# Cross-attention scores of one head on one half of the partitions

## The chip, the core and the metric

The kernel runs on one core of one Trainium2 chip. The time is the device time of one execution in microseconds. PE is TensorE (matmuls), PEld its weight loads, DVE VectorE, ACT ScalarE, POOL GpSimd, SP the engine that issues most DMAs. All five run their own instruction streams and wait for each other by semaphores.

## The reference

One decoder layer on x of 32 batch rows x 112 tokens x 256 channels: a first attention (a delta rule with an MLP), then cross-attention to a context of 375 keys, then a routed MLP with six experts. The change touches the middle part alone:

```python
Q, K, V = split(query @ wq.T), split(key @ wk.T), split(value @ wv.T)   # 16 heads of 16 channels
scores = einsum('bhqd,bhkd->bhqk', Q, K) / sqrt(16)
scores = where(mask == 1, -1e9, scores)
out = einsum('bhqk,bhkd->bhqd', softmax(scores), V)                     # then w_out
```

## The kernel before

The order of the instructions on each engine is written by hand; there is no scheduler. After the first attention (to about 500 us) comes the cross-attention, a loop over the batch rows (32 of them, three to a round of the hardware loop, `par` being the place in the round), then the routed MLP from about 1100 us.

**How a batch row goes through it.** Three rows are in work at once. While row b has its scores and weighted values, row b+1 (`nxt`) has the maxima of its scores, row b+2 (`far`) its projections of k, q and v, and row b-1 (`prev`) its last weighted values, its transposes and its output projection. `step(t, par)` in the stream of PE, ACT, DVE, POOL and SP writes one such mixed row.

**Exact products in fp32r.** Each of q and k is split in a high and a low part, and the score is hi·hi + hi·lo + lo·hi. SP copies the parts by DMA into stacks so that one matmul sums all three (`spread_heads`, L454 to L465). The stack `kst` holds a *pair* of heads on 96 partitions (3 terms x 2 heads x 16 channels) and 376 keys. The stack `qst` holds each head alone on the same 96 partitions with zeros at the other head's, so that products with the pair's keys give one head. Partition 96 holds ones in `kst` and the negated row maximum in `qst`, which `spread_max` (L467 to L470) brings by a DMA from `negm`.

**Slots.** The scores come transposed, keys on partitions, in 12 slots `q` of a row: 3 pieces of 125 keys x 4 groups of 4 heads, each 448 columns in one of PSUM banks 0, 1, 2. For a slot PE runs one bf16 product that adds a large negative number at masked keys (`mask_scores`, L968 to L976; it waits until the exponentials have freed the bank), then two products of 224 columns, one for each pair of heads (`score`, L978 to L983). ACT takes the exponential of the slot (`exponentials`, L1431) into one of six buffers `pr`, and `weighted_values` (L985 to L997) multiplies it with the values: four heads, on four strips of 32 output partitions of bank 6; each of these fp32 matmuls is two instructions in the trace. These run in three groups of four slots.

**Maxima.** The maximum over the keys of each head of the next row: PE computes 112 x 376 scores of one head (`row_max`, L950 to L961) into bank 4 or 5, DVE adds the mask's bias and reduces (`maxima`, L1822 to L1831). The 16 heads are spread over slots 0 to 7 by the table `MAXIMA` (L80). PE transposes the 16 maxima (`transpose_max`), ACT negates them (`negate_max`), SP spreads them.

**Clearing.** POOL clears `qst` and sets `kst`'s last partition to one, once for each of the three stacks (`clear_stack`, L568 to L572), the first inside the first attention, the other two at its end.

Of the kernel before, what the change touches and what calls it, by code (L numbers as in the profile page):

```python
# [40 lines left out]
P = 128  # L41
# [28 lines left out]
PROBS = 6  # L70
# [3 lines left out]
ROWS = 3 * 2 * HD  # L74
# [5 lines left out]
MAXIMA = ((0, 1, 0, 0), (1, 1, 1, 0), (1, 1, 0, 1), (0, 1, 0, 0), (1, 1, 0, 0), (1, 1, 1, 0), (1, 0, 0, 1), (0, 1, 0, 0))  # L80
# [36 lines left out]
def decoder_layer(nc, io, out):  # L117
    with ExitStack() as ctx:
# [74 lines left out]
        with ExitStack() as scope:  # L193
# [116 lines left out]
        def pair(stack, n):  # L310

            return stack[:, n % PPC, n // PPC]

        def head(stack, hd):

            return pair(stack[:, hd % 2], hd // 2)

        def both(stack, n):

            return stack[:, :, n % PPC, n // PPC]  # L320
# [28 lines left out]
        def heads_at(q, place):  # L349

            n = sum(sum(x) for x in MAXIMA[:q]) + sum(MAXIMA[q][:place])
            return range(n, n + MAXIMA[q][place])

# [16 lines left out]
        def filled(stack, t):  # L370

            return {"kst": 48, "qst": 96}[stack] * (t + 1)
# [29 lines left out]
        def _(sp):  # L402
# [51 lines left out]
            def spread_heads(t, par):  # L454

                b = t * RB + par
                for src, r, ready in ((khi, 0, "k_hi"), (khi, 2, "k_hi"), (klo, 1, "k_lo")):
                    sp.wait_ge(s2[ready], DC * (b + 1))
                    dst = kst[par][r:ROWS:3]
                    sp.dma_start(dst.bitcast(F32), src[:].bitcast(F32)).then_inc(s2[f"kst{par}"], 16)  # L460
                for src, r, ready in ((qhi, 0, "q_hi"), (qhi, 1, "q_hi"), (qlo, 2, "q_lo")):
                    sp.wait_ge(s2[ready], b + 1)
                    for e in range(2):
                        dst = qst[par][3 * e + r:ROWS:6, e]
                        sp.dma_start(dst.bitcast(F32), src[cols(e, P // 2)].bitcast(F32)).then_inc(s2[f"qst{par}"], 16)  # L465

            def spread_max(t, par):  # L467
                b = t * RB + par
                sp.wait_ge(s2["negm"], b + 1)
                sp.dma_start(qst[par][ROWS:ROWS + 1].bitcast(F32), negm[:].bitcast(F32)).then_inc(s2["negm_in"], 16)  # L470
# [70 lines left out]
        def _(pool):  # L541
# [26 lines left out]
            def clear_stack(i):  # L568
                nc.gpsimd.memset(qst[i][0:ROWS].bitcast(F32), 0.0).then_inc(s2["cleared"], 1)
                pool.wait_ge(s2["cleared"], 2 * i + 1)  # L570
                nc.gpsimd.memset(kst[i][ROWS:ROWS + 1].bitcast(F32), 1.0).then_inc(s2["cleared"], 1)
                pool.wait_ge(s2["cleared"], 2 * i + 2)  # L572

            def stack_constants():

                pool.wait_ge(s["y_ps"], G)
                clear_stack(0)
# [64 lines left out]
            pool.wait_ge(s["x_mlp"], G)  # L642
            clear_stack(1)
# [65 lines left out]
        def _(pe):  # L709
# [240 lines left out]
            def row_max(t, par, heads):  # L950

                n = t * RB + par
                for hd in heads:
                    if hd == 0:
                        pe.wait_ge(s2[f"qst{par}"], filled("qst", t))
                        pe.wait_ge(s2[f"kst{par}"], filled("kst", t))
                        if not is_row(n, 0):
                            pe.wait_ge(s2["negm"], n)
# [9 lines left out]
            def mask_scores(t, par, q):  # L968

                b = t * RB + par  # L970
                if q == 0:
                    pe.wait_ge(s2["negm_in"], 16 * (b + 1))
# [5 lines left out]
            def score(t, par, q, i):  # L978

                n = HPB // 2 * (q % HPB) + i  # L980
                mm = pe.matmul(bank[q % 3][0:KP, cols(i, 2 * T)], pair(kst[par], n)[:, cols(q // HPB, KP)], both(qst[par], n), start=False, stop=True, skip_group_check=True)  # L981
                if i == HPB // 2 - 1:
                    mm.then_inc(s2["sc_ps"], 1)  # L983

            def weighted_values(t, par, q):  # L985
# [6 lines left out]
                for i in range(HPB):  # L992
                    hd = HPB * (q % HPB) + i
                    row = 2 * HD * i
                    mm = pe.matmul(bank[6][row:row + 2 * HD, cols(hd // HPB)], vaug[par][:, c3, hd], pr[q % PROBS][:, i],  # L995
# [29 lines left out]
            def step(t, par, first=False, following=2):  # L1025

                prev, nxt, far = ahead(t, par, -1), ahead(t, par, 1), ahead(t, par, 2)
                for q in range(SLOTS):

                    maxima = following >= 1 and q < len(MAXIMA)  # L1030
                    mask_scores(t, par, q)
                    for i in range(HPB // 2):
                        score(t, par, q, i)
                        if maxima:
                            row_max(*nxt, heads_at(q, i))
                    if q % HPB == 1 and q > HPB:
                        for earlier in range(q - HPB - 1, q - 1):
                            weighted_values(t, par, earlier)
                    elif q == 1 and not first:
                        for earlier in range(SLOTS - HPB, SLOTS):  # L1040
                            weighted_values(*prev, earlier)
                    if maxima:
                        row_max(*nxt, heads_at(q, 2))
                    if q in (1, 2) and following >= 2 and not first:
                        project_k(*far, q - 1)
                    if q == 3 and not first:
                        transpose_o(*prev)
                    if q == 4 and following >= 2:
                        transpose_h(*far)
                    if q == 5 and not first:  # L1050
                        transpose_on(*prev)
                    if q == 6 and following >= 2:
                        project_q(*far)
                    if q == 7 and not first:
                        project_out(*prev)
                    if maxima:
                        row_max(*nxt, heads_at(q, 3))
                    if q == 8 and following >= 1:
                        transpose_max(*nxt)
                    if q == 8 and following == 0:  # L1060
                        transpose_group(0)
                    if q == 8 and following >= 2:
                        project_v(*far, 0)
                        project_v(*far, 1)


# [199 lines left out]
        def _(act):  # L1266
# [188 lines left out]
            def step(t, par, first=False, following=2, context=True):  # L1455
                prev, nxt, far = ahead(t, par, -1), ahead(t, par, 1), ahead(t, par, 2)
                for q in range(SLOTS):
                    exponentials(t, par, q)
                    if q == 1 and not first:
                        copy_pv(*prev)  # L1460
                    if q in (1, 2) and following >= 2:
                        high_k(*far, q - 1)
                    if q == 4 and following >= 2:
                        copy_h(*far)
                    if q == 5 and not first:
                        copy_on(*prev)
                    if q == 6 and following >= 2:
                        high_q(*far)
                    if q == 8 and following >= 1:
                        negate_max(*nxt)  # L1470
                    if q == 8 and following >= 2:
                        copy_v(*far, 0)
                    if q == 9 and following >= 2:
                        copy_v(*far, 1)
                    if q == 9 and context:
                        high_context(*ahead(t, par, 3))
                    if q == 9 and following == 0:
                        keep_h(0)
# [125 lines left out]
        def _(dve):  # L1604
# [217 lines left out]
            def maxima(t, par, heads):  # L1822
                n = t * RB + par
                for hd in heads:
                    if hd == 0:
                        dve.wait_ge(s2["flags"], n + 1)
                    if hd >= 2:
# [3 lines left out]
                                                   op0=ALU.add, op1=ALU.max, accum_out=head(smax, hd).unsqueeze(1)).then_inc(s2["smax"], 1)  # L1831
# [26 lines left out]
            def step(t, par, first=False, following=2, norm=True):  # L1858
                prev, nxt, far = ahead(t, par, -1), ahead(t, par, 1), ahead(t, par, 2)
                for q in range(SLOTS):  # L1860
                    if following >= 1 and q < len(MAXIMA):
                        for place in range(3):
                            maxima(*nxt, heads_at(q, place))
                    if q in (2, 3) and following >= 2:
                        low_k(*far, q - 2)
                    if q == 4 and not first:
                        normalise_heads(*prev)
                    if q == 7 and following >= 2:
                        low_q(*far)
                    if following >= 1 and q < len(MAXIMA):  # L1870
                        maxima(*nxt, heads_at(q, 3))
                    if q == 7 and not first:
                        add_row(*prev)
# [278 lines left out]
```

## Time and profile before

| | us |
|---|---|
| median of 3 runs | 1502.91 (1502.6 to 1508.58) |
| the profiled execution | 1504.27 |
| its span | 1502.4 |
| PE busy | 1315.5 (88%) |
| DVE busy | 907.6 (60%) |
| ACT busy | 646.6 (43%) |
| POOL busy | 420.7 (28%) |

The page cuts the span in 40 slices of 37.6 us and gives the busy share and the granted TensorE clock of each; the cross-attention is slices 14 to 29. Matmuls overlap in the array, and their ends are modelled: the duration of one is longer than what it takes of PE's time in a full queue. That is read from the distance between starts or ends.

### The profile page before, as it was taken

Reading aid. Unit: us, or ns where it says so; the run is one execution under the profiler, and the core shown is the slowest. Engines: PE = TensorE matmul, PEld = TensorE weight load, DVE = VectorE, ACT = ScalarE, POOL = GpSimd, SP = SyncE. Lnnn points to the kernel's source line nnn. Section 1 sums busy time; section 2 is a strip of 40 time slices with the busy share of each in tenths; the row PEclk is TensorE's granted clock in tenths of the full one; section 3 lists DMA queues with packets and bytes.
Section 4 is the critical chain, followed back from the end, with each engine's and each line's share of the span. In section 5 each row is a group of like instructions: output and inputs, shape, how many; then the busy total and the mean of one; then the engine's idle time right before and its main releaser. Section 6 shows DMA issues by size and latency. Waiting matters only on the chain.

```text
span 1502.4 us, 33730 instructions
## 1 busy us (share of the span) xinstructions
PE 1315.5 (88%) x11138; PEld 1182.9 (79%) x11138; DVE 907.6 (60%) x2823; ACT 646.6 (43%) x1474; POOL 420.7 (28%) x387
## 2 busy tenths in 40 slices
PE   4999999999897699999999999999975518988987
PEld 4888998998786588888888888888865417877887
DVE  4676567557545366666666666666557534544567
ACT  3533434334332255555555555555542204544532
POOL 2233223224312311111111111111006662323453
PEclk9999999999998699999999999999985558999999
DMA  7699100000002445454555555554304322322264
GB/s 182 149 236 247 32 0 0 0 0 0 18 13 49 126 110 114 115 116 120 120 120 119 119 122 119 120 120 117 79 9 126 116 76 70 101 80 86 89 160 138
DMA packets 117837, 143.96 MB, mean 96 GB/s; under 512 B 24112, under 2 KB 101280, under 8 KB 117744
## 3 DMA queue, kind: packets, MB, share of 16 engines
q1 hardware_dynamic: 111024, 127.21, 36.1%
q0 software_dynamic: 6160, 15.69, 3.2%
q8 instruction: 43, 0.70, 0.2%
q14 instruction: 34, 0.28, 0.1%
q10 hardware_dynamic: 576, 0.07, 0.0%
HBM read 75.61 MB, written 42.15 MB: 78 GB/s over the span
## 4 chain that ended last, share of the span: by engine, by line
PE 59%; issue 14%; POOL 9%; DVE 8%; SPq 2%; DMA 2%; ACT 2%; another core or an unknown queue 0%; POOLq 0%; DVEq 0%; ACTq 0%
PE psum L725 19%; PE psum L961 7%; PE psum L995 5%; PE psum L976 5%; PE psum L981 5%; POOL routed_y L686 4%; POOL routed_h L671 3%; PE psum L846 2%; SPq L465 2%; PE psum L843 2%; PE psum L832 2%; PE psum L933 2%; PE psum L1022 2%; PE psum L714 1%; PE psum L1008 1%
## 5 line engine op out<-in xcount | busy, mean ns | idle before, releaser
L1830 DVE CUSTOM_DVE_ANT_0 junk<-psum,biasq 112x375 f32<-112x375 f32 x512 | 270.0, 546 | 116.5 <-PE psum L961 78.2
L1435 ACT ACTIVATE pr<-psum 125x448 f32<-125x448 f32 x384 | 202.7, 544 | 115.5 <-PE psum L981 107.1
L981 PE MATMUL psum<-qst,kst 97*125 97x224 f32 x768 | 225.8, 353 | 0.0
L961 PE MATMUL psum<-kst,qst 96*112 96x376 f32 x512 | 185.7, 371 | 12.4 <-DVE smax L1830 10.7
L981 PEld LDWEIGHTS psum<-qst,kst 97*125 97x125 f32 x768 | 146.2, 190 | 8.0
L976 PE MATMUL psum<-flagk,negbig 125*125 125x448 bf16 x384 | 139.0, 362 | 4.0 <-DMA qst<-negm 3.8
L566 POOL TENSOR_TENSOR rs<-rs,neg_half 112x1 f32<-112x1 f32 x32 | 18.3, 571 | 388.1 <-DVE rs L1808 388.1
L961 PEld LDWEIGHTS psum<-kst,qst 96*112 96x112 f32 x512 | 91.3, 179 | 41.9 <-DVE smax L1830 36.7
L686 POOL DMA_INDIRECT routed_y<-yb,yrow x61 | 59.3, 972 | 136.5 <-ACT yb L1565 134.8
L995 PE MATMUL psum<-pr,vaug 125*32 125x112 f32 x3072 | 93.7, 262 | 0.0
L995 PEld LDWEIGHTS psum<-pr,vaug 125*32 125x32 f32 x3072 | 70.3, 109 | 15.4 <-issue 6.1
L631 POOL TENSOR_SCALAR biasq<-maskq 112x375 f32<-112x375 int32 x32 | 56.0, 1749 | 89.8 <-PE psum L981 89.8
L1697 DVE TENSOR_TENSOR clo<-ctxT,chi 128x750 fp32r<-128x750 f32 x32 | 30.1, 941 | 81.1 <-ACT chi L1337 81.1
L2075 DVE TENSOR_TENSOR hidb<-sgb,psum 128x256 f32<-128x256 f32 x61 | 25.7, 421 | 88.2 <-ACT sgb L1550 83.7
L671 POOL DMA_INDIRECT routed_h<-h,slot x64 | 63.6, 993 | 36.5 <-DVE slot L1982 18.8
L1356 ACT COPY xq<-psum 112x224 f32<-112x224 f32 x96 | 32.6, 348 | 88.1 <-PE psum L832 85.6
L832 PE MATMUL psum<-tri,cT 112*112 112x112 f32 x384 | 48.4, 268 | 19.3 <-DVE triT L1711 10.8
L587 POOL TENSOR_TENSOR cT<-negT,masks_sb 112x448 f32<-112x448 f32 x48 | 61.2, 1303 | 7.9 <-DVE negT L1706 7.9
L832 PEld LDWEIGHTS psum<-tri,cT 112*112 112x112 f32 x384 | 44.5, 181 | 23.2 <-POOL cT L587 13.3
L976 PEld LDWEIGHTS psum<-flagk,negbig 125*125 125x125 bf16 x384 | 52.8, 137 | 12.4 <-issue 5.3
L1550 ACT ACTIVATE sgb<-psum 128x256 f32<-128x256 f32 x61 | 23.5, 385 | 75.4 <-PE psum L1124 75.4
L714 PE MATMUL psum<-ident_sb,h 112*128 112x112 f32 x128 | 21.5, 330 | 38.8 <-DVE h L1855 25.9
(308 smaller groups left out, 3443.5 us busy)
## 6 DMA issues: line engine op xcount, KB each, us to landing
kst<-khi SPq DMA_DIRECT2D x64, 376.0 KB, 5.5
routed_h<-in_route_pad SPq DMA_DIRECT2D x6, 3640.0 KB, 41.1
kst<-klo SPq DMA_DIRECT2D x32, 376.0 KB, 6.7
ctxT<-in_ctxT SPq DMA_DIRECT2D x32, 375.0 KB, 5.2
hblk<-routed_h SPq DMA_DIRECT2D x61, 130.0 KB
qst<-qhi SPq DMA_DIRECT2D x128, 56.0 KB, 2.2
h<-routed_y SPq DMA_DIRECT2D x16, 448.0 KB, 5.2
stage<-in_e SPq DMA_DIRECT2D x21, 256.0 KB
```

The lines of the kernel that those rows point to most:

```text
L587: nc.gpsimd.tensor_tensor(cT[:, n], negT[:], over_rows(M_BT + 1 + n), op=ALU.mult).then_inc(s["cmask"], 1)
L631: nc.gpsimd.tensor_scalar(biasq[:, par, :], maskq[:], 1.0, -BIG, ALU.is_equal, ALU.mult)
L671: pool.indirect_dma_start(hbuf[:, :], to, h3[g % RINGS][:, j, :], None).then_inc(s3[f"scat{g % RINGS}"], 16)
L686: pool.indirect_dma_start(ybuf[:, :], to, yb[:, u], None).then_inc(s4[f"out{u}"], 16)
L725: mm = pe.matmul(to, st, mv, start=n == 0, stop=n == len(products) - 1)
L832: mm = pe.matmul(bank[6 + u][0:T, cols(j % 2)], cT[:, n, j], tri[:, j], start=True, stop=True)
L961: pe.matmul(bank[max_bank(n, hd)][0:T, 0:S2E], head(qst[par][0:ROWS], hd), pair(kst[par][0:ROWS], hd // 2), start=True, stop=True).then_in ...
L976: pe.matmul(bank[q % 3][0:KP, 0:GT], negbig[:], flags, start=True, stop=False, skip_group_check=True)
L981: mm = pe.matmul(bank[q % 3][0:KP, cols(i, 2 * T)], pair(kst[par], n)[:, cols(q // HPB, KP)], both(qst[par], n), start=False, stop=True, s ...
L995: mm = pe.matmul(bank[6][row:row + 2 * HD, cols(hd // HPB)], vaug[par][:, c3, hd], pr[q % PROBS][:, i], start=q == 0, stop=c3 == KC - 1, s ...
L1435: nc.scalar.activation(pr[q % PROBS][:].rearrange("k i q -> k (i q)"), bank[q % 3][0:KP, 0:GT], ACT.Exp, scale=1.0 / HD ** 0.5).then_inc(s ...
L1830: nc.vector.tensor_tensor_reduce(out=junk[:, hd % 2, :], in0=bank[max_bank(n, hd)][0:T, 0:S2], in1=biasq[:, par, :], scale=1.0, scalar=-3e ...
```

## The change

A stack holds one head on 48 partitions now (3 terms x 16 channels), even heads at partitions 0 to 47, odd ones at 64 to 111, in `kst` and `qst` alike. The row of ones and of the maximum is at partition 48 of each half. `qst` has no zeros and is half as large.

- A slot is four heads of one parity: slot q has parity q % 2 (`head_of`). Its scores are four products of 49 partitions x 112 columns instead of two of 97 x 224.
- Slots go two and two: both masks, four products of the even slot, four of the odd one (`scores`). All 12 slots are in six such blocks.
- The maxima of a pair of heads stand side by side, on two halves and in two banks, and wait once for all maxima before them; eight pairs stand between the blocks, and the table is gone.
- SP issues six DMAs for `kst` (three before) and two for `negm` (one before). The order of channels in `xwk` and of `xwo`'s rows follows.
- POOL sets 32 partitions of each half of `kst` to one, and clears nothing.
- The other steps of a row (projections, transposes, copies) are the same instructions at other places.

```diff
-ROWS = 3 * 2 * HD
+TERMS = 3
+ROWS = TERMS * HD
+HALF = 64
...
-                qst[i] = w2(f"qst{i}", [ROWS + 1, 2, PPC, DC, T], F32R)
-                kst[i] = w2(f"kst{i}", [ROWS + 1, PPC, DC, S2E], F32R)
+                qst[i] = w2(f"qst{i}", [P, PPC, DC, T], F32R)
+                w2(f"gap_q{i}", [P, PPC, DC, T])
+                kst[i] = w2(f"kst{i}", [P, PPC, DC, S2E], F32R)
...
+        def rows_of(e, first, n):
+
+            return slice(HALF * e + first, HALF * e + first + n)
+
+        def head(stack, hd, rows):
+
+            n = hd // 2
+            return stack[rows_of(hd % 2, 0, rows), n % PPC, n // PPC]
+
+        def head_of(q, i):
+
+            n = HPB * (q % HPB // 2) + i
+            return 2 * n + q % 2
...
-                    dst = kst[par][r:ROWS:3]
-                    sp.dma_start(dst.bitcast(F32), src[:].bitcast(F32)).then_inc(s2[f"kst{par}"], 16)
+                    for e in range(2):
+                        dst = kst[par][rows_of(e, HD * r, HD)]
+                        sp.dma_start(dst.bitcast(F32), src[cols(e, P // 2)].bitcast(F32)).then_inc(s2[f"kst{par}"], 16)
...
-                nc.gpsimd.memset(qst[i][0:ROWS].bitcast(F32), 0.0).then_inc(s2["cleared"], 1)
-                pool.wait_ge(s2["cleared"], 2 * i + 1)
-                nc.gpsimd.memset(kst[i][ROWS:ROWS + 1].bitcast(F32), 1.0).then_inc(s2["cleared"], 1)
-                pool.wait_ge(s2["cleared"], 2 * i + 2)
+                for e in range(2):
+                    nc.gpsimd.memset(kst[i][rows_of(e, HALF // 2, HALF // 2)].bitcast(F32), 1.0).then_inc(s2["cleared"], 1)
+                    pool.wait_ge(s2["cleared"], 2 * i + e + 1)
...
+                else:
+                    pe.wait_ge(s2["smax"], HEADS * n + heads[0])
                 for hd in heads:
...
-                    if hd >= 2:
-                        pe.wait_ge(s2["smax"], HEADS * n + hd - 1)
-                    pe.matmul(bank[max_bank(n, hd)][0:T, 0:S2E], head(qst[par][0:ROWS], hd), pair(kst[par][0:ROWS], hd // 2), start=True, stop=True).then_inc(s2["max_ps"], 1)
+                    pe.matmul(bank[max_bank(n, hd)][0:T, 0:S2E], head(qst[par], hd, ROWS), head(kst[par], hd, ROWS), start=True, stop=True).then_inc(s2["max_ps"], 1)
...
-                n = HPB // 2 * (q % HPB) + i
-                mm = pe.matmul(bank[q % 3][0:KP, cols(i, 2 * T)], pair(kst[par], n)[:, cols(q // HPB, KP)], both(qst[par], n), start=False, stop=True, skip_group_check=True)
-                if i == HPB // 2 - 1:
+                hd = head_of(q, i)
+                mm = pe.matmul(bank[q % 3][0:KP, cols(i)], head(kst[par], hd, ROWS + 1)[:, cols(q // HPB, KP)], head(qst[par], hd, ROWS + 1), start=False, stop=True, skip_group_check=True)
+                if i == HPB - 1:
                     mm.then_inc(s2["sc_ps"], 1)
...
+                def maxima(n):
+                    if following >= 1:
+                        row_max(*nxt, range(2 * n, 2 * n + 2))
+
+                def scores(q):
                     mask_scores(t, par, q)
-                    for i in range(HPB // 2):
+                    mask_scores(t, par, q + 1)
+                    for i in range(HPB):
                         score(t, par, q, i)
...
+                    for i in range(HPB):
+                        score(t, par, q + 1, i)
```

PE's whole row is now, in this order: maxima 0; k projection 0 (of `far`); scores 0 and 1; maxima 1; weighted values 8 to 11 of `prev`; scores 2, 3; maxima 2; k projection 1; maxima 3; `transpose_o`; scores 4, 5; maxima 4; `transpose_h`; weighted values 0 to 3; `transpose_on`; maxima 5; scores 6, 7; maxima 6; q projection; output projection; scores 8, 9; maxima 7; v projection; `transpose_max`; scores 10, 11; weighted values 4 to 7.

On PE, in the loop of the cross-attention, slots 2 and 3 of a row stood like this before (the second half of the k projection lies between them; 125x224 is a score product, 112x376 a maximum, 125x448 a mask):

```order
L976 MATMUL psum<-flagk,negbig 125x448
L981 MATMUL psum<-qst,kst 125x224
L960 REGISTER_ALU
L961 MATMUL psum<-kst,qst 112x376
L981 MATMUL psum<-qst,kst 125x224
L960 REGISTER_ALU
L961 MATMUL psum<-kst,qst 112x376
L725 MATMUL psum<-chi,wxk_hi 128x376 x2
L725 MATMUL psum<-clo,wxk_hi 128x376 x2
L725 MATMUL psum<-chi,wxk_lo 128x376 x2
```

The same place of the changed kernel:

```order
L979 MATMUL psum<-flagk,negbig 125x448
L977 REGISTER_ALU
L979 MATMUL psum<-flagk,negbig 125x448
L984 MATMUL psum<-qst,kst 125x112 x8
L962 REGISTER_ALU
L964 MATMUL psum<-kst,qst 112x376 x2
L728 MATMUL psum<-chi,wxk_hi 128x376 x2
L728 MATMUL psum<-clo,wxk_hi 128x376 x2
L728 MATMUL psum<-chi,wxk_lo 128x376 x2
L962 REGISTER_ALU
L964 MATMUL psum<-kst,qst 112x376 x2
```

Two masks stand together, the products are eight in a row with half the columns each, and the maxima come two at a time behind them. Products on half of the partitions (125x112, 112x376) border on ones over the whole array at three places here.

On SP, one row of the loop before:

```order
L460 DMA kst<-khi 32x4x752 x2
L460 DMA kst<-klo 32x4x752
L465 DMA qst<-qhi 16x4x224 x4
L465 DMA qst<-qlo 16x4x224 x2
L470 DMA qst<-negm 1x16x112
```

And now:

```order
L460 DMA kst<-khi 16x4x752 x4
L460 DMA kst<-klo 16x4x752 x2
L465 DMA qst<-qhi 16x4x224 x4
L465 DMA qst<-qlo 16x4x224 x2
L472 DMA qst<-negm 1x8x112 x2
```

The bytes are the same, in 14 transfers instead of 10.

## Rows read from the trace of the kernel before

**Rows 1.** The page: busy us, share of the span and instructions by engine.

```profile
PE 1315.5 (88%) x11138; PEld 1182.9 (79%) x11138; DVE 907.6 (60%) x2823; ACT 646.6 (43%) x1474; POOL 420.7 (28%) x387
```

**Rows 2.** The page: granted TensorE clock in 40 slices, in tenths.

```profile
PEclk9999999999998699999999999999985558999999
```

**Rows 3.** Stretches of 100 us: busy by engine, PEclk, DMA share, GB/s.

```profile
core 0: us, PE busy (x) PEld busy (x) DVE busy (x) ACT busy (x) POOL busy (x), PEclk, DMA share, GB/s
...
700.00:800.00 100.00, 98.65 (x1071) 87.40 (x1069) 66.09 (x226) 56.08 (x119) 17.35 (x16) 1.00 0.52 117
```

**Rows 4.** Groups of lines, shapes apart, 600 to 1056 us; columns as the page's part 5.

```profile
L1830 DVE CUSTOM_DVE_ANT_0 junk<-psum,biasq 112x375 f32<-112x375 f32 x391 | 206.3, 546 | 76.5 <-PE psum L961 65.4 <-issue 4.8
L981 PE MATMUL psum<-qst,kst 97*125 97x224 f32 x583 | 170.7, 350 | 0.0
...
L961 PE MATMUL psum<-kst,qst 96*112 96x376 f32 x391 | 140.0, 365 | 5.6 <-DVE smax L1830 5.6
...
L976 PE MATMUL psum<-flagk,negbig 125*125 125x448 bf16 x292 | 104.5, 358 | 1.4 <-DMA qst<-negm 1.4
L995 PE MATMUL psum<-pr,vaug 125*32 125x112 f32 x2336 | 71.1, 262 | 0.0
```

**Rows 5.** Timeline of PE, 816 to 819 us: start, duration, engine, line, count.

```profile
816.36 0.54 PE L981 MATMUL psum<-qst,kst 97*125 97x224 f32 x2
816.83 0.97 PE L995 MATMUL psum<-pr,vaug 125*32 125x112 f32 x32
817.73 0.40 PE L976 MATMUL psum<-flagk,negbig 125*125 125x448 bf16 x1
...
818.19 0.35 PE L976 MATMUL psum<-flagk,negbig 125*125 125x448 bf16 x1
818.22 0.54 PE L981 MATMUL psum<-qst,kst 97*125 97x224 f32 x2
818.60 0.35 PE L976 MATMUL psum<-flagk,negbig 125*125 125x448 bf16 x1
```

**Rows 6.** Timeline of PE: q projection, router products; then these alone by stretch.

```profile
811.19 1.05 PE L933 MATMUL psum<-h2T,xwq_sb 128*128 128x112 f32 x8
...
1110.99 1.65 PE L1083 MATMUL psum<-router_sb,hall 128*112 128x6 f32 x16
...
core 0: us, PE busy (x) PEld busy (x), PEclk, DMA share, GB/s
1110.90:1112.60 1.70, 1.61 (x16) 1.64 (x16) 1.00 0.00 0
```

**Rows 7.** Timeline of PE: maxima between products, 800 to 802 us.

```profile
800.80 0.34 PE L961 MATMUL psum<-kst,qst 96*112 96x376 f32 x1
800.97 0.27 PE L981 MATMUL psum<-qst,kst 97*125 97x224 f32 x1
801.47 0.42 PE L961 MATMUL psum<-kst,qst 96*112 96x376 f32 x1 [0.23 <-DVE smax L1830]
```

**Rows 8.** Timeline of PE's weight loads around weighted values, 801 and 817 us.

```profile
801.82 0.73 PEld L995 LDWEIGHTS psum<-pr,vaug 125*32 125x32 f32 x32 [0.18 <-ACT pr L1435]
802.72 0.17 PEld L961 LDWEIGHTS psum<-kst,qst 96*112 96x112 f32 x1 [0.17 <-DVE smax L1830]
...
817.73 0.13 PEld L976 LDWEIGHTS psum<-flagk,negbig 125*125 125x125 bf16 x1 [0.17 <-issue]
```

**Rows 9.** Waits, 600 to 1056 us: total us, times, longest us.

```profile
PE psum L961 <- DVE smax L1830: 5.6, 24, 0.2
```

**Rows 10.** Timeline: SP's issues of one row, and the mask product after them.

```profile
619.03 1.23 SPq L460 DMA_DIRECT2D kst<-khi  x2
620.48 0.55 SPq L460 DMA_DIRECT2D kst<-klo  x1
625.26 2.48 SPq L465 DMA_DIRECT2D qst<-qhi  x4
627.78 1.24 SPq L465 DMA_DIRECT2D qst<-qlo  x2
629.07 1.28 SPq L470 DMA_DIRECT2D qst<-negm  x1
...
631.69 0.40 PE L976 MATMUL psum<-flagk,negbig 125*125 125x448 bf16 x1 [0.32 <-DMA qst<-negm]
```

**Rows 11.** Timeline of POOL: one stack cleared, before the first rows.

```profile
496.34 1.59 POOL L569 MEMSET qst<- 96x1792 f32 x1 [19.67 <-DVE x_res L1692]
497.99 2.60 POOL L571 MEMSET kst<- 1x3008 f32 x1
```

More of the change, by code:

```diff
@@ L347, in ring_turn @@
             return 16 * (i // RINGS + 1)
-        def heads_at(q, place):
-            n = sum(sum(x) for x in MAXIMA[:q]) + sum(MAXIMA[q][:place])
-            return range(n, n + MAXIMA[q][place])
         def max_bank(row, hd):
@@ L370, in filled @@
         def filled(stack, t):
-            return {"kst": 48, "qst": 96}[stack] * (t + 1)
+            return 16 * 2 * TERMS * (t + 1)
         def split_weights():
@@ L642, in _ @@
             pool.wait_ge(s["x_mlp"], G)
+            pool.wait_ge(s2["flags"], 2)
             clear_stack(1)
@@ L992, in weighted_values @@
                 for i in range(HPB):
-                    hd = HPB * (q % HPB) + i
                     row = 2 * HD * i
-                    mm = pe.matmul(bank[6][row:row + 2 * HD, cols(hd // HPB)], vaug[par][:, c3, hd], pr[q % PROBS][:, i],
+                    mm = pe.matmul(bank[6][row:row + 2 * HD, cols(q % HPB)], vaug[par][:, c3, head_of(q, i)], pr[q % PROBS][:, i],
                                    start=q == 0, stop=c3 == KC - 1, skip_group_check=True)
@@ L1033, in step @@
                         score(t, par, q, i)
[L1034 to L1055, printed above, removed]
@@ new lines, in step @@
+                maxima(0)
+                if following >= 2 and not first:
+                    project_k(*far, 0)
+                scores(0)
+                maxima(1)
+                if not first:
+                    for q in range(SLOTS - HPB, SLOTS):
+                        weighted_values(*prev, q)
+                scores(2)
+                maxima(2)
+                if following >= 2 and not first:
+                    project_k(*far, 1)
+                maxima(3)
+                if not first:
+                    transpose_o(*prev)
@@ new lines, in step @@
+                scores(4)
+                maxima(4)
+                if following >= 2:
+                    transpose_h(*far)
+                for q in range(HPB):
+                    weighted_values(t, par, q)
+                if not first:
+                    transpose_on(*prev)
+                maxima(5)
+                scores(6)
+                maxima(6)
+                if following >= 2:
+                    project_q(*far)
+                if not first:
+                    project_out(*prev)
@@ L1067, in transpose_group @@
+                scores(8)
+                maxima(7)
+                if following >= 2:
+                    project_v(*far, 0)
+                    project_v(*far, 1)
+                if following >= 1:
+                    transpose_max(*nxt)
+                else:
+                    transpose_group(0)
+                scores(10)
+                for q in range(HPB, 2 * HPB):
+                    weighted_values(t, par, q)
             def transpose_group(g):
@@ L1456, in step @@
                 prev, nxt, far = ahead(t, par, -1), ahead(t, par, 1), ahead(t, par, 2)
[L1457 to L1478, printed above, removed]
+                if following >= 2:
+                    high_k(*far, 0)
+                exponentials(t, par, 0)
+                exponentials(t, par, 1)
+                if not first:
+                    copy_pv(*prev)
+                exponentials(t, par, 2)
+                exponentials(t, par, 3)
+                if following >= 2:
+                    high_k(*far, 1)
+                exponentials(t, par, 4)
+                exponentials(t, par, 5)
+                if following >= 2:
+                    copy_h(*far)
+                if not first:
+                    copy_on(*prev)
+                exponentials(t, par, 6)
+                exponentials(t, par, 7)
+                if following >= 2:
+                    high_q(*far)
+                exponentials(t, par, 8)
+                exponentials(t, par, 9)
+                if following >= 2:
+                    copy_v(*far, 0)
+                    copy_v(*far, 1)
+                if following >= 1:
+                    negate_max(*nxt)
+                if context:
+                    high_context(*ahead(t, par, 3))
+                if following == 0:
+                    keep_h(0)
+                exponentials(t, par, 10)
+                exponentials(t, par, 11)
             def last_mlp(m):
@@ L1859, in step, with largest @@
                 prev, nxt, far = ahead(t, par, -1), ahead(t, par, 1), ahead(t, par, 2)
[L1860 to L1873, printed above, removed]
+                def largest(n):
+                    if following >= 1:
+                        maxima(*nxt, range(2 * n, 2 * n + 2))
+                largest(0)
+                if following >= 2:
+                    low_k(*far, 0)
+                largest(1)
+                largest(2)
+                if following >= 2:
+                    low_k(*far, 1)
+                largest(3)
+                if not first:
+                    normalise_heads(*prev)
+                largest(4)
+                largest(5)
+                largest(6)
+                if following >= 2:
+                    low_q(*far)
+                if not first:
+                    add_row(*prev)
+                largest(7)
                 if norm:
```

43 lines of the change are left out of this document (14 added, 29 removed).

## The prediction

> **What bounds the kernel now.** I read first the busy times of the page: PE is busy 88% of the span, DVE 60% [rows 1]. Then the slices: the stretch from about 530 to 1090 us, the cross-attention over the 32 batch rows, holds a full TensorE clock [rows 2], and the table by stretches shows PE at 98.6 of 100 us there [rows 3]. The grouped lines from 600 to 1056 us hold 391 maxima products [rows 4], 16 to a batch row, so 24.4 rows in 456 us: 18.7 us a row. What the change rewrites on PE are the groups L981 (scores), L961 (maxima); L976 (mask) and L995 (weighted values) stand around them [rows 4]. DVE needs about 0.55 us for each maximum, 16 a row or some 9 us of 18.6, so it isn't the bound. The page's means of a matmul (350, 365 ns) are latencies; what one costs in a full queue is the distance between starts or ends in the timeline, and I price by that. At the granted clock of 1.00 a column takes 1/2.4 ns, so 448 mask columns take 0.187 us.
>
> **Score products.** A mask and its two products repeat every 0.41 us (818.19 to 818.60) [rows 5]. Less the mask that is 0.22, so 0.11 us a product, though its 224 columns stream in 0.093. What holds it is the weight load of 125 columns: router products that stream only 6 columns after loading 112 cost (1.65-0.17)/15 = 0.099 us each at full clock, and the q projection with 128 loaded and 112 streamed (1.05-0.26)/7 = 0.113 [rows 6]. For 125 columns that gives 0.110. The change doubles the products (24 to 48 a row), halves what each streams (112 columns, 0.047 us), and leaves each its own load of 125 columns. So a product on the same half still costs 0.11. Eight of them now follow two masks. Three gaps lie within the even four, three within the odd four: 6 x 0.11. Between the fourth even and first odd product the halves differ, so the odd load can run early: 0.05; the last streams 0.05. Sum 0.76 against 4 x 0.11 = 0.44 now: +0.32, six times a row +1.9, times 32 rows **+61 us**. Bounds: strictly one load after another, 0.88 a block, +84; loads of the two halves wholly beside each other, 0.44 a block, 0.
>
> **Maxima.** One costs 0.17 us today (800.80 to the next start at 800.97) [rows 7]. A pair now lies on two halves and two banks. No row of before shows two row halves at work together; the nearest shows four column strips at once: 32 instructions of L995 that would stream 0.093 us each alone (fp32 goes twice over its 112 columns: the q projection's 0.113 has the same stream) pass in (0.97-0.26)/31 = 0.023 us, a quarter, and their loads keep up [rows 5, 8]. So I take a pair at 0.19 instead of 0.34: -0.15, eight times, 31 rows: **-37 us**. Bounds: 0.17 a pair, -42; the second load (0.099) after the first, 0.27 a pair, -17. PE also stops once a row for the previous maximum, 5.6 us in 24.4 rows, 0.23 each [rows 9]. A pair now waits for both maxima before it, with everything else of PE queued behind that wait; but the pairs lie further apart: the tightest place, pairs 2 and 3, has a projection of k between them (six products of 376 columns, 1.0 us) against two maxima on DVE at 0.55 each [rows 4]; with the pair itself before it that just fits. **-7 us**.
>
> **Changes of the array's shape.** Around each group of L995 the weight loads stand idle 0.17 us, put down to issue or to a semaphore that was long there [rows 8]. In time of PE: from the end of the products (816.36+0.54 = 816.90) to the end of the next mask (817.73+0.40 = 818.13) lie 1.23 us; 32 instructions at 0.023 make 0.73, the mask 0.19. So entering and leaving cost 0.31, or 0.15 a change [rows 5]. Today a row has six such changes. Afterwards products on 49 or 48 partitions stand between ones on 112 to 128: counted in the order, 21 borders a row between whole array, half rows and column strips (every block of scores and every lone pair of maxima has two). The Trainium skill, "TensorEngine Tiling (Array Packing)", section Key Properties, says that a change of tiling mode, not of tile, drains TensorE. The trace agrees for column strips by the 0.17 us of idle load; for row halves nothing here shows it; with the rule the sum holds the next term, without it not. The nearest row being the column strips, I price all: 15 more x 0.15 = 2.25 us, 32 rows: **+72 us**. Bounds: 0 and about 90 (0.19, should each one cost like the dearer of the two sides).
>
> **Everything else.** The exponentials and mask products keep their number. DVE, ACT and POOL have free time, and their moved steps keep their slack while a row gets longer. The k stack goes out in six transfers instead of three, the negated maxima in two instead of one. An issue takes SP about 0.62 us, the one of negm 1.28 [rows 10]. SP is idle for much of a row; only negm is late already, by 0.32 us in the row shown. The new order has 16 transposed maxima later by a v projection (2.2 us) but two slots of scores, the weighted values, a pair and half a k projection follow before the next masks. I take 0 and keep +25 us as the bound (0.8 a row, one more small issue). POOL's clearing goes from 1.59 + 2.60 to two of 2.60 us a stack, +1.0; two such stacks hold up row 1's start, one more the stage before [rows 11], and SP's three further issues there cost 1.9: **+5 us**, bounds 0 and 7.
>
> **Sum.** 61 - 37 - 7 + 72 + 5 = +94 us. The profiled execution took 1504.27 us, 1.87 over its span, and gives 1598; the median of the runs, 1502.91, gives 1597, which I forecast.
>
> **Rivals.**
> 1. Changing between whole array and row halves is free. For it: no row shows its price. Then +94 - 72 = +22: 1525, between 1510 and 1555.
> 2. Faster: a queue that loads the odd half's weights under the even four wholly, and no price for changes. One mechanism, the two halves as two independent arrays, at each block of eight. Then products cost 0 more, maxima -42, the stop -7, start +5: -44, so 1459. It decides from a block of eight under 0.44 + 44/192 = 0.67 us, 0.084 a product. For it: column strips do run four at once. Against: there, neighbours in the order lie on different strips; here four neighbours lie on the same half, and matmuls would have to overtake. The Trainium skill, "TensorE: Matmul & The Clock Gate", section The mechanism, has matmuls start and end in program order, which speaks against it; the trace has no overtaking matmul. By that page the block would be no shorter than the 0.76 above.
> 3. No side by side at all to speak of: blocks 0.88 (+84), pairs 0.27 (-17), stop -7, changes +72, start +5: +137, 1640. For it: nothing shows row halves overlapping. A late negm on top of the forecast gives 1622 and counts here.
> 4. It nets to nothing: halfway between rivals 1 and 2 in the products (blocks of about 0.65 us) with free changes, 1503 within 7 us.
>
> **How the numbers follow.** Forecast 0.50 (own range 1560 to 1635), rival 1 0.20, rival 2 0.10, rival 3 0.15, nothing 0.05. A change under 0.5% (7.5 us) can't be told from none here. Slower: 0.50 + 0.20 + 0.15 and nearly all of it beyond 0.5%, less a little of rival 1's low end: 0.84. Within 0.5%: 0.05. Faster: rival 2 and that end, 0.11. The range drops rival 2 and the tail of rival 3: 1512 to 1645.
>
> **What would show it.** In the profile after: distances between starts of the scores products near 0.11 us within a four; the two maxima of a pair starting within some 0.02 us of each other (forecast) or 0.1 and more apart (rival 3); idle weight loads of 0.17 us at every border of shapes (forecast) or only around the weighted values (rival 1); a row of about 21.4 us (forecast), 19.2 (rival 1), 17.2 (rival 2). PE stays over 90% busy between 530 us and the end of the stage. The forecast is wrong if a block of eight takes under 0.6 us, or if the row's time grows by waits of PE for DVE, ACT or SP instead.

## The result and the profile after

| | before | changed |
|---|---|---|
| median, us | 1502.84 | 1646.39 (1639.83 to 1660.58, 4 runs) |
| ratio | | 1.096, interval 1.088 to 1.104 |
| profiled execution, its span | 1504.27, 1502.4 | 1643.54, 1641.7 |

The change costs 144 us; I had forecast 94, and the measured median lies 1.4 us above my range. The direction came true and two thirds of the amount, but not for the reasons given, so the parts matter more than the total. One of the four runs of `spread` below (1568.1 us) was in a slower state of the chip, and its ratio is that of the other three, whose median is 1555.47.

The page of the changed kernel, busy times and clock, answers to [rows 1, 2]:

```profile
PE 1412.3 (86%) x11906; PEld 1163.7 (71%) x11906; DVE 909.3 (55%) x2823; ACT 635.2 (39%) x1474; POOL 435.8 (27%) x387
...
PEclk9999999999976898997997999999965556999999
```

The clock no longer stands at full speed through the cross-attention. Four stretches of it (PE, PEld, DVE, ACT, POOL busy with counts, clock, DMA share, GB/s), against [rows 3]:

```profile
725.00:750.00 25.00, 23.30 (x256) 17.47 (x255) 15.07 (x52) 11.61 (x25) 3.84 (x4) 1.00 0.75 106
750.00:775.00 25.00, 23.67 (x190) 16.59 (x188) 10.12 (x34) 8.35 (x19) 3.77 (x3) 0.58 0.56 85
775.00:800.00 25.00, 24.74 (x253) 18.18 (x253) 14.55 (x50) 11.43 (x25) 3.81 (x3) 0.94 0.51 89
800.00:825.00 25.00, 22.59 (x275) 16.73 (x274) 14.58 (x48) 12.88 (x28) 5.73 (x5) 1.00 0.72 103
```

PE is busy for 94% instead of 98.6, the clock falls to 0.58 in one of four stretches, and the DMA engines are busy for 0.51 to 0.75 at 85 to 106 GB/s, where 0.52 moved 117 before.

The clock has two levels, 1.2 and 2.4 GHz, and 0.58 is a mixture of them. It fell right behind a stop of PE of 1.33 us (for q's low part, up to 753.43); then PE worked for 23.3 us without a pause at the lower level:

```profile
754.30:777.60 23.30, 23.30 (x149) 16.19 (x147) 9.07 (x34) 6.43 (x14) 0.46 (x1) 0.50 0.51 83
```

One row in PE's timeline (start, duration, line, count), against [rows 5, 7]:

```profile
802.04 0.97 PE L997 MATMUL psum<-pr,vaug 125*32 125x112 f32 x32
804.38 0.42 PE L964 MATMUL psum<-kst,qst 48*112 48x376 f32 x2 [1.37 <-DMA qst<-qlo]
804.73 0.62 PE L728 MATMUL psum<-chi,wxk_hi 128*128 128x376 f32 x2
805.19 0.51 PE L728 MATMUL psum<-clo,wxk_hi 128*128 128x376 f32 x2
805.53 0.51 PE L728 MATMUL psum<-chi,wxk_lo 128*128 128x376 f32 x2
...
806.35 0.66 PE L984 MATMUL psum<-qst,kst 49*125 49x112 f32 x8
806.83 0.39 PE L964 MATMUL psum<-kst,qst 48*112 48x376 f32 x2
...
812.02 0.66 PE L984 MATMUL psum<-qst,kst 49*125 49x112 f32 x8
812.76 0.42 PE L964 MATMUL psum<-kst,qst 48*112 48x376 f32 x2
...
815.58 0.66 PE L984 MATMUL psum<-qst,kst 49*125 49x112 f32 x8
816.39 0.43 PE L964 MATMUL psum<-kst,qst 48*112 48x376 f32 x2 [0.16 <-DVE smax L1859]
...
825.57 0.42 PE L964 MATMUL psum<-kst,qst 48*112 48x376 f32 x2 [1.35 <-DMA qst<-qlo]
```

Four things are to be seen. First, PE stands still for 1.37 us in front of the first pair of maxima, for the transfer of q's low part, and again 21.2 us later; that is a row at full clock, 18.69 before. Secondly, the block of eight products takes 0.48 us (806.35 to 806.83), not the 0.76 I had summed. Thirdly, two 376-column products of the k projection after a pair of maxima take 0.46 us to the next start (804.73 to 805.19) against 0.34 for the next two. Fourthly, at two places the pair of maxima starts 0.74 and 0.81 us after the eight products instead of 0.48: a wait for DVE of 0.26 and 0.33 us. The profile's own figure for it, 0.16, counts only from the modelled end of the products, which is later than the moment at which PE could have gone on.

PE's weight loads in the same block, against [rows 8], show how a block can be so short:

```profile
806.35 0.52 PEld L984 LDWEIGHTS psum<-qst,kst 49*125 49x125 f32 x8 [0.33 <-issue]
```

Eight loads of 125 columns lie in 0.52 us. Between 806.35 and 806.38 two of them have started, by 806.50 four: one load of each half every 0.11 us, (0.52-0.19)/3. So the even and the odd products run in pairs, though the program has four even ones first. In front of the block PE's loads stand idle for 0.33 us, which takes in the streaming of the second mask.

The waits of PE, 650 to 1130 us (total us, times, longest), against [rows 9]:

```profile
PE psum L964 <- DMA qst<-qlo: 26.0, 19, 1.8
...
PE psum L964 <- DVE smax L1859: 3.1, 20, 0.2
```

Of the page, part 5 (the last figure is the idle time put down to the transfer in the whole kernel):

```profile
L964 PE MATMUL psum<-kst,qst 48*112 48x376 f32 x512 | 113.4, 436 | 58.4 <-DMA qst<-qlo 45.7
```

And the transfers of 700 to 900 us in both kernels (count, KB each, median us from issue to landing). Before:

```profile
q1 hardware_dynamic: 18323, 23.22, 53.3%
...
kst<-khi SPq DMA_DIRECT2D x21, 376.0 KB, 5.8
...
qst<-qhi SPq DMA_DIRECT2D x44, 56.0 KB, 2.4
```

After:

```profile
q1 hardware_dynamic: 14950, 18.77, 61.9%
...
kst<-khi SPq DMA_DIRECT2D x32, 188.0 KB, 5.5
...
qst<-qhi SPq DMA_DIRECT2D x36, 56.0 KB, 5.0
...
qst<-qlo SPq DMA_DIRECT2D x18, 56.0 KB, 4.1
```

A transfer of q lands 5.0 us after its issue instead of 2.4. Engine time for a MB, over all transfers of the queue: 0.533 x 16 x 200 / 23.22 = 73 us before, 0.619 x 16 x 200 / 18.77 = 106 us after. The k transfers hold half of the bytes each and still take as long.

### The profile page after: what moved, and what is told of

Same layout as the page of the kernel before. It is cut to its first block and busy times, and to the rows that moved or that the text cites. A ratio compares the mean times of both kernels' runs of the same rounds, so it can differ in the third digit from the quotient of the medians.

```text
span 1641.7 us, 35236 instructions
## 1 busy us (share of the span) xinstructions
PE 1412.3 (86%) x11906; PEld 1163.7 (71%) x11906; DVE 909.3 (55%) x2823; ACT 635.2 (39%) x1474; POOL 435.8 (27%) x387
## 5 line engine op out<-in xcount | busy, mean ns | idle before, releaser
L1453 ACT ACTIVATE pr<-psum 125x448 f32<-125x448 f32 x384 | 188.0, 542 | 209.7 <-PE psum L984 197.6
L984 PEld LDWEIGHTS psum<-qst,kst 49*125 49x125 f32 x1536 | 112.5, 205 | 75.5 <-issue 75.5
L964 PE MATMUL psum<-kst,qst 48*112 48x376 f32 x512 | 113.4, 436 | 58.4 <-DMA qst<-qlo 45.7
L984 PE MATMUL psum<-qst,kst 49*125 49x112 f32 x1536 | 139.2, 302 | 0.0
L979 PE MATMUL psum<-flagk,negbig 125*125 125x448 bf16 x384 | 123.0, 406 | 0.0
L964 PEld LDWEIGHTS psum<-kst,qst 48*112 48x112 f32 x512 | 49.8, 187 | 90.9 <-DMA qst<-qlo 30.9
L633 POOL TENSOR_SCALAR biasq<-maskq 112x375 f32<-112x375 int32 x32 | 69.0, 2155 | 30.3 <-PE psum L984 30.3
L1428 ACT CAST khi<-psum 128x376 fp32r<-128x376 f32 x64 | 30.1, 472 | 113.6 <-PE psum L728 100.6
L1845 DVE TENSOR_TENSOR klo<-psum,khi 128x376 fp32r<-128x376 f32 x64 | 35.0, 549 | 48.1 <-ACT khi L1428 48.1
L728 PE MATMUL psum<-chi,wxk_hi 128*128 128x376 f32 x128 | 44.5, 433 | 13.7 <-DVE clo L1726 13.3
```

The lines of the kernel that those rows point to most:

```text
L633: nc.gpsimd.tensor_scalar(biasq[:, par, :], maskq[:], 1.0, -BIG, ALU.is_equal, ALU.mult)
L728: mm = pe.matmul(to, st, mv, start=n == 0, stop=n == len(products) - 1)
L964: pe.matmul(bank[max_bank(n, hd)][0:T, 0:S2E], head(qst[par], hd, ROWS), head(kst[par], hd, ROWS), start=True, stop=True).then_inc(s2["max ...
L979: pe.matmul(bank[q % 3][0:KP, 0:GT], negbig[:], flags, start=True, stop=False, skip_group_check=True)
L984: mm = pe.matmul(bank[q % 3][0:KP, cols(i)], head(kst[par], hd, ROWS + 1)[:, cols(q // HPB, KP)], head(qst[par], hd, ROWS + 1), start=Fals ...
L1453: nc.scalar.activation(pr[q % PROBS][:].rearrange("k i q -> k (i q)"), bank[q % 3][0:KP, 0:GT], ACT.Exp, scale=1.0 / HD ** 0.5).then_inc(s ...
```

## The experiments

**1. Spread the destinations.** The changed kernel writes each term of 16 channels to 16 adjacent partitions, the kernel before to every third (k) or sixth (q). `spread` puts the terms of a channel side by side within a half:

```diff
-                        dst = kst[par][rows_of(e, HD * r, HD)]
+                        dst = kst[par][HALF * e + r:HALF * e + ROWS:TERMS]
...
-                        dst = qst[par][rows_of(e, HD * r, HD)]
+                        dst = qst[par][HALF * e + r:HALF * e + ROWS:TERMS]
```

> The changed kernel with one edit: within each half the three terms of a channel lie side by side (partition 3 x channel + term), so that each transfer of 16 partitions is spread over 48 instead of lying on 16 adjacent ones. Theory N (writes to 16 adjacent partitions are slow, the queue of k and q transfers runs late, and PE waits about 1.3 us a row for qst and then gets a lower clock): PE's idle time before maxima 0 falls under 0.1 us a row, the clock stays at 1.00 between 600 and 1000 us, a row takes about 19.9 us, the kernel about 1545. Rival T (14 issues instead of 10 make it late) and rival O (the new order has k and q ready too late): nothing changes, about 1640.

Measured: 1558.85 us (median of four, 1544.72 to 1568.1; 1555.47 without the slowest), ratio to before 1.030 (1.024 to 1.037). A row takes 19.88 us (median distance of the starts of `transpose_max` between 600 and 1100 us; 18.69 in the kernel before, and so for every row below). The stretch of 700 to 800 us, the transfers, and what is left of the wait:

```profile
700.00:800.00 100.00, 98.51 (x1124) 72.32 (x1123) 63.19 (x215) 50.73 (x111) 19.01 (x15) 1.00 0.45 112
```
```profile
q1 hardware_dynamic: 17891, 22.40, 44.4%
...
kst<-khi SPq DMA_DIRECT2D x40, 188.0 KB, 3.7
...
qst<-qhi SPq DMA_DIRECT2D x43, 56.0 KB, 2.0
```
```profile
PE psum L964 <- DMA qst<-qlo: 1.2, 2, 0.8
```

The clock is back at 1.00, q lands in 2.0 us, a MB costs 0.444 x 16 x 200 / 22.40 = 63 us, and the wait came twice in 400 us. Theory N holds and T and O fall: the places of the destinations are 87 to 91 us of the 144 (against 1558.85 and 1555.47).

**2. The same from the other side.** `before_six` splits the k transfers of the kernel before into six and leaves them spread; `before_narrow` does the same and lays them on 16 adjacent partitions (the number of landings that PE waits for follows in both):

```diff
-                    dst = kst[par][r:ROWS:3]
+                    for e in range(2):
+                        dst = kst[par][48 * e + r:48 * e + 48:3]              # before_six
+                        dst = kst[par][32 * r + 16 * e:32 * r + 16 * e + 16]  # before_narrow
...
-                        dst = qst[par][3 * e + r:ROWS:6, e]
+                        dst = qst[par][32 * r + e:32 * r + 32:2, e]           # before_narrow
```

> The kernel before with its three k transfers a row split into six of 16 partitions each, still every third partition. Theory N: no change beyond 0.5%, 1503 to 1510, PE's wait for qst stays rare. Rival T: the number of transfers is what costs, over 1520.

> The same six transfers, but each on 16 adjacent partitions (terms one after another in blocks of 32 partitions), q on every second of 32. Theory N: engine time per MB of the DMAs goes up as in the changed kernel (by a third or more against before_six), the landing of q goes from about 2.4 to 4 us or more; the spare time of about 1 us a row is used up, so 1520 to 1580. Rival T or O: as before_six.

Measured: `before_six` 1502.6, ratio 0.999 (0.997 to 1.001); `before_narrow` 1575.13, ratio 1.047 (1.043 to 1.051). The number of transfers costs nothing that can be told, their place 5%. The narrow one's transfers and wait, 600 to 1000 us:

```profile
q1 hardware_dynamic: 33763, 42.55, 69.0%
...
kst<-klo SPq DMA_DIRECT2D x38, 188.0 KB, 8.4
```
```profile
PE psum L977 <- DMA qst<-negm: 28.9, 19, 2.5
```

Here the wait shows at negm's transfer, which stands behind q's in the queue: 28.9 us in 19 rows, 1.52 a row; its row takes 20.32 us, 1.63 more than before. A MB costs 0.69 x 16 x 400 / 42.55 = 104 us against 68 in `before_six` (0.502, 47.55 MB).

**3. The order of the products.** `spread_alternate`:

```diff
                     for i in range(HPB):
                         score(t, par, q, i)
-                    for i in range(HPB):
                         score(t, par, q + 1, i)
```

> The spread kernel with the eight products of a block in the order even, odd, even, odd. Theory P (the two halves take their products from the stream independently: the trace of the changed kernel has loads in pairs every 0.11 us though four even ones precede four odd ones): same time as spread within 0.3%, the block of eight 0.45 to 0.5 us. Rival (order counts at the edges, half a gap a block): 0.05 us x 192, 10 us faster.

Measured: 1560.55 (1557.61 to 1566.2), its row 19.84 us against 19.88. The order within a block makes no difference that can be told.

**4. The halves apart.** `spread_apart` puts the second mask between the fours:

```diff
                     mask_scores(t, par, q)
-                    mask_scores(t, par, q + 1)
                     for i in range(HPB):
                         score(t, par, q, i)
+                    mask_scores(t, par, q + 1)
```

> The spread kernel with the second mask of a block between the four even and the four odd products, so that the halves never have products side by side. Theory P (halves side by side halve the cost; a product alone costs one load of 125 columns, 0.11 us): each four takes 0.44 instead of a block of eight taking 0.48, and two more borders a block: 6 x (0.40 + 0.38) = +4.7 us a row, the kernel near 1705. Rival (loads on half rows are twice as fast for themselves, 0.055 each, side by side or not): only the borders, +2.3 a row, near 1630.

Measured: 1682.15 (two runs), row 23.22: +3.3 us a row. The sum of theory P, +4.7, overstates it by 1.4. The timeline:

```profile
812.12 0.64 PE L984 MATMUL psum<-qst,kst 49*125 49x112 f32 x4
812.69 0.40 PE L979 MATMUL psum<-flagk,negbig 125*125 125x448 bf16 x1
813.02 0.31 PE L984 MATMUL psum<-qst,kst 49*125 49x112 f32 x1
813.03 0.42 PE L964 MATMUL psum<-kst,qst 48*112 48x376 f32 x1
813.18 0.49 PE L984 MATMUL psum<-qst,kst 49*125 49x112 f32 x3
```

Four products alone take (0.64-0.31)/3 = 0.11 us each, as one load of 125 columns does, so a half row is not faster by itself and the rival falls. The *even* maximum, which stands behind the four odd products, starts at 813.03 beside the first of them: it overtook three matmuls.

The overtaking does not explain the 1.4 us, though. A block costs about 0.70 us more than in `spread` with a pair of maxima behind it (from the start of the k projection to the weighted values: 813.81 - 810.70 = 3.11 against 2.41) and just as much without one (from `transpose_max` to the weighted values: 809.39 - 807.54 = 1.85 against 1.16). That is 0.08 less than the 0.78 of the sum, six times. The other part is that PE now comes late enough for DVE: the two waits of 0.26 and 0.33 us are gone, and some 0.1 us at each of two further places.

**5. The price of a border.** `before_borders` moves a maximum of the kernel before into the middle of two groups of weighted values, four more borders a row:

```diff
-                        for earlier in range(q - HPB - 1, q - 1):
+                        for earlier in range(q - HPB - 1, q - 3):
                             weighted_values(t, par, earlier)
...
                     if maxima:
                         row_max(*nxt, heads_at(q, 2))
+                    if q % HPB == 1 and q > HPB:
+                        for earlier in range(q - 3, q - 1):
+                            weighted_values(t, par, earlier)
```

(and the same for the group of `prev` at q == 1).

> The kernel before with a maximum moved into the middle of two of the three groups of weighted values: four more borders a row between whole array and column strips, all else the same. Theory B: 0.15 to 0.19 us each, a row from 18.66 to 19.3 or 19.4, the kernel at 1522 to 1527. Rival F: 1503.

Measured: 1526.68, ratio 1.017 (1.014 to 1.020); row 19.50 against 18.69, which makes 0.20 us a border if all of it is borders. But the second of the moved maxima also waits for DVE. PE and its loads at the two places:

```profile
810.14 0.59 PE L995 MATMUL psum<-pr,vaug 125*32 125x112 f32 x16
810.66 0.42 PE L961 MATMUL psum<-kst,qst 96*112 96x376 f32 x1
...
817.90 0.59 PE L995 MATMUL psum<-pr,vaug 125*32 125x112 f32 x16
818.63 0.42 PE L961 MATMUL psum<-kst,qst 96*112 96x376 f32 x1
```
```profile
810.66 0.17 PEld L961 LDWEIGHTS psum<-kst,qst 96*112 96x112 f32 x1 [0.17 <-issue]
...
818.63 0.17 PEld L961 LDWEIGHTS psum<-kst,qst 96*112 96x112 f32 x1 [0.38 <-DVE smax L1836]
```

The same 16 instructions take 0.52 us to the next start at the first place and 0.73 at the second. Less these 0.21 us of waiting a row grew by 0.60, 0.15 us a border, as theory B had it.

`spread_more` adds five borders of row halves to `spread`, `spread_fewer` takes two away:

```diff
                 scores(8)
-                maxima(7)
                 if following >= 2:
                     project_v(*far, 0)
+                maxima(7)
+                if following >= 2:
                     project_v(*far, 1)
```

(one of the three moves of `spread_more`; the others put maxima 1 between the second and third slot of the weighted values, and maxima 4 behind `transpose_h`.) In `spread_fewer` the order behind maxima 4 is weighted values, maxima 5, `transpose_h`, `transpose_on`.

> The spread kernel with the same instructions and five more borders a row between half rows and other shapes: maxima 1 in the middle of the weighted values, maxima 4 behind transpose_h, maxima 7 in the middle of the v projection. Theory B (each border costs PE about 0.19 us, of half rows as of column strips): a row grows from 19.85 to 20.8 us, the kernel by 29 us over spread. Rival F (borders of row halves are free, the row grew by something else): no change.

> The spread kernel with two borders a row fewer: weighted values, maxima 5, transpose_h and transpose_on in this order behind maxima 4. Theory B: -0.38 us a row, less up to 0.2 where maxima 5 come early for DVE, so a row of 19.5 to 19.65 and the kernel 6 to 12 us faster than spread. Rival F: no change, or slower by the wait.

Measured: `spread_more` 1605.64, 47 us above `spread`, row 21.31, +1.43. But half of that is new waits, not borders:

```profile
PE psum L969 <- DVE smax L1863: 5.2, 14, 0.4
...
PE psum L728 <- DVE clo L1730: 4.7, 14, 0.4
```

In 14 rows 5.2 us (maxima 7 too late for `transpose_max`) and 4.7 us (the low part of the context too late), 0.71 a row. The other 0.72 are 0.14 a border. Where nothing waits, from the products of scores 8 to the last two products before `transpose_max`, `spread` needs 801.80 - 799.02 = 2.78 us and this one 818.71 - 815.60 = 3.11: 0.16 for each of two borders. `spread`, then `spread_more`:

```profile
799.02 0.66 PE L984 MATMUL psum<-qst,kst 49*125 49x112 f32 x8
...
801.80 0.40 PE L728 MATMUL psum<-wxv_hi,clo 128*125 128x256 f32 x2
```
```profile
815.60 0.66 PE L984 MATMUL psum<-qst,kst 49*125 49x112 f32 x8
...
818.71 0.40 PE L728 MATMUL psum<-wxv_hi,clo 128*125 128x256 f32 x2
819.48 0.26 PE L969 MATMUL psum<-ident_sb,smax 112*16 112x112 f32 x1 [0.37 <-DVE smax L1863]
```

`spread_fewer`: 1552.68 (1548.64 to 1555.36), row 19.65, -0.23. It gains two borders and pays for a wait for DVE at maxima 5: 1.34 us from the start of the weighted values to it (810.82 to 812.16) where 0.90 is usual, so 0.44; a wait of 0.33 at maxima 6 goes. That leaves 0.34 for two borders, 0.17 each. The ratio intervals of its total and that of `spread` overlap; the row tells them apart. So a border of row halves costs 0.14 to 0.17 us on the average of these places. That they cost nothing (F) is out.

No version of the changed kernel here beats the kernel before; the nearest, `spread` and `spread_fewer`, are 3.0 and 3.4% slower, with intervals that overlap.

## Why the prediction was right or wrong

- **Everything else: the step that failed.** I priced the six transfers by their issues and took 0 for the rest, with 25 us as bound. I looked at how many bytes and issues there are, and not at which partitions they go to, though the diff changes that from every third to 16 adjacent ones. It costs 87 to 91 us (1646.4 against 1558.9 or 1555.5), over three times the bound. The direct wait is about 38 of them: the page has 45.7 us of it, and 7.8 of these stand in front of the first row. About 6 lie in the start (below). The rest goes with rows in which the clock was not full: between 600 and 1100 us half of the rows of the changed kernel take about 21.2 us, two with a long stretch at the lower level 31.1, and the mean is 22.8 (clock 0.58 to 0.94 in the stretches above; 1.00 in all of `spread`'s from 600 to 1100). That the stop makes the clock fall is argued from their order in time; not every stop was followed by a fall (the one of 1.37 us up to 804.38 was not: 1.00 from 800 to 825 us). What I had named as a sign of being wrong, a row that grows by waits of PE, is what came. The Trainium skill has a mechanism that would do it, "SBUF — State Buffer", section Door 1: The DMA port swizzle: bandwidth goes by how many of 16 ports the partitions reach, and four adjacent partitions share one; by it 16 adjacent ones reach four. The runs agree in direction (106 and 104 us a MB narrow, 63 to 73 spread); that ports are the mechanism no run here shows.
- **Score products, +61: wrong, +8 measured.** The price of one load, 0.11, was right (experiment 4). That the odd four can't start before the even four are through was not: a block costs 0.48 instead of 0.44, 0.04 x 192 = 8 us. I had the mechanism as rival 2 and gave it 0.10, arguing from program order, and a block under 0.6 us was my other sign of being wrong.
  The Trainium skill, "TensorE: Matmul & The Clock Gate", section The mechanism, has matmuls start and end in program order; between two row halves the trace of `spread_apart` contradicts it (813.03 before 813.18).
- **Maxima, -37:** the two loads of a pair start together (0.17 to 0.19 us for both), as taken. From the start of an isolated pair to the next start it is 0.35 (804.38 to 804.73), the border behind it included.
- **The stop for DVE, -7: did not come.** A pair waits for both maxima before it, and DVE had not finished them at two places: 0.26 and 0.33 us a row above. The kernel before lost 0.40 in front of one maximum by the same measure (800.97 to 801.47, less 0.10), not the 0.23 that I read [rows 7, 9].
- **Changes of shape, +72: right.** 21 borders a row stand in the order, and row halves pay for them as column strips do: 0.14 to 0.17 and 0.15 us in experiment 5, where I took 0.15 for both. By the row it fits: 18.69 - 1.2 (maxima) + 0.24 (blocks) + 15b = 19.88 gives b = 0.14.
- **Start, +5:** the first mask starts at 526.8 instead of 514.2, +12.6. POOL's four memsets take 10.6 us instead of 8.4, but 6.3 are q's transfers again (a wait of 7.82 instead of 1.54); in `spread` it is at 520.3.

So the total came near by luck, by two errors of opposite sign: 53 us too much for the products, 87 to 91 too few for the transfers. The row of 21.2 us at full clock, so close to the 21.4 that I had named, is the same luck.

Without its slow transfers, in `spread`, the change costs 53 to 56 us. In the traces only 31 of them lie in the 30 rows between the second and the last `transpose_max` (542.6 to 1137.9 us against 530.7 to 1095.3). The start up to there takes 12 more, and the end of the stage, up to the first router product, 11 more (26.4 us instead of 15.7). I had no term for the end. In both stretches `spread` had the lower clock for a part of the time where the kernel before had the full one (0.82 against 1.00 from 537 to 553 us). At the end, `spread`, then before:

```profile
1138.00:1164.40 26.40, 24.23 (x255) 17.98 (x254) 4.20 (x16) 9.33 (x19) 1.04 (x1) 0.61 0.01 2
```
```profile
1095.30:1111.00 15.70, 14.57 (x231) 12.44 (x230) 4.56 (x17) 10.25 (x21) 1.04 (x1) 1.00 0.01 3
```

At the end it fell behind a stop of 1.52 us for negm's transfer (up to 1141.55), where the one of the kernel before was 0.47. No run here separates these causes.

## What to carry to other kernels

Packing two small matmuls into halves of the array pays only if whole stretches stay in that shape: each change costs about 0.15 us here, and a lone pair of 376-column products has two of them around it for the 0.15 that it saves. When a change moves data to other partitions, look at the transfers' destinations as well as at their bytes. And look at what waits for the queue's last transfer. When a wait is to be told from a border, compare starts: the idle time that the profile gives counts from a modelled end, and here it showed 0.16 us of a wait of 0.33.

## What was not expected of the hardware

- Two row halves take their matmuls from PE's stream independently: products 5 to 8 run beside 1 to 4, and a maximum overtakes three products of the other half (813.03). Each half alone keeps to 0.11 us for a load of 125 columns.
- With k written to 16 adjacent partitions a transfer, the queue as a whole took 104 to 106 us of engine time a MB; with k on every third partition 63 to 73.
- A border between shapes costs PE 0.15 us for column strips (`before_borders`) and 0.14 to 0.17 for row halves (`spread_more`, `spread_fewer`).
- Stops of 1.3 to 1.4 us a row go together with 25 us stretches at clock 0.58 to 0.94 in the changed kernel; `before_narrow`, with 1.4 to 1.5 us of idle a row, had 0.95 to 1.00 in its 100 us stretches from 600 to 1100.
